# A graph network on one core: row indices of gathers copied by GpSimd, one attention product with the weights' columns, tables of pairs made in two places

## What is computed

```python
# layer 0: attention over the edges and the nodes' own loops, 4 heads of 128
alpha = leaky_relu(a_src[src] + a_dst[dst] + a_edge)
ex = exp(alpha - segment_max(alpha, dst)[dst])
out = segment_sum(h[src] * (ex / segment_sum(ex, dst)[dst])[:, :, None], dst) + bias
# layer 1: two convolutions, 256 and 512 wide
x = segment_sum((x @ W1)[src] * norm[:, None], dst) + b1     # then relu, and again with W2
# layer 2
x_neigh = segment_sum(x[src] * edge_weight[:, None], dst) / max(degree, 1)
out = x @ W_self.T + b_self + x_neigh @ W_neigh.T + b_neigh
# layer 3: the sum goes over the edges by the other end
out = segment_sum((x @ W3)[by] * edge_weight[:, None], to) + bias
```

## Time and profile before

| | |
|---|---|
| median of 3 runs | 4595.86 us (4595.8 to 4596.43) |
| the profiled execution | 4594.67 us, span 4592.7 us |
| PE busy | 3095.3 us (67%) |
| GpSimd (POOL) busy | 2949.3 us (64%) |
| VectorE (DVE) busy | 2564.1 us (56%) |
| ScalarE (ACT) busy | 1715.2 us (37%) |
| mean granted TensorE clock | 0.803 of 2.4 GHz |

### The profile page before, as it was taken

How to read it: one execution, slowest core, us unless ns; L and a number is a source line. 1 busy time by engine, 2 the same in 40 slices (tenths; PEclk the granted TensorE clock), 3 DMA queues, 4 the chain that set the end, 5 groups by cost and what they waited for, 6 DMA issues and landing times. The chain is left out here.

```text
span 4592.7 us, 69306 instructions
## 1 busy us (share of the span) xinstructions
PE 3095.3 (67%) x12429; PEld 1743.1 (38%) x12430; DVE 2564.1 (56%) x4877; ACT 1715.2 (37%) x3843; POOL 2949.3 (64%) x3208
## 2 busy tenths in 40 slices
PE   6577674487788666665545665776777799577773
PEld 6344442355556243333323333332222244222221
DVE  9456565666666663334443444665656654556556
ACT  1111110355555553333323333324444433344444
POOL 8667776666666566666666666666666667566662
PEclk8677776699998886666756666898999999789996
DMA  3211111355555153332343333325666611466663
GB/s 101 74 45 63 63 48 37 129 164 160 162 160 156 44 148 88 89 88 87 86 139 90 88 87 87 75 66 165 176 172 176 174 51 43 132 172 177 174 176 127
DMA packets 207412, 520.84 MB, mean 113 GB/s; under 512 B 63334, under 2 KB 70638, under 8 KB 206892
## 3 DMA queue, kind: packets, MB, share of 16 engines
q0 software_dynamic: 157600, 413.73, 32.3%
q1 hardware_dynamic: 49714, 105.90, 7.3%
HBM read 475.94 MB, written 43.49 MB: 113 GB/s over the span
## 5 line engine op out<-in xcount | busy, mean ns | idle before, releaser
L1554 PE MATMUL g_part<-g_rows,g_hot 128*128 x3328 | 1564.1, 619 | 868.9 <-SPq L1467 459.8
L1536 DVE TENSOR_TENSOR k_acc<-k_acc,g_part 128x256 f32 (+1 forms) x1664 | 920.3, 553 | 1046.0 <-PE g_part L1554 404.1
L1554 PEld LDWEIGHTS g_part<-g_rows,g_hot 128*128 128x128 f32 x3328 | 753.1, 245 | 1679.7 <-issue 1610.8
L1489 ACT ACTIVATE g_rows<-g_rows,k_rec 128x256 f32<-128x256 f32 (+1 forms) x1176 | 663.6, 577 | 1094.8 <-PE g_part L1554 277.0
L1166 POOL DMA_INDIRECT at_rows<-h_table,at_index x392 | 395.7, 1010 | 260.4 <-ACTq L1189 151.6
L1505 POOL DMA_INDIRECT g_rows<-support,g_index x392 | 377.2, 962 | 227.7 <-issue 125.2
L1505 POOL DMA_INDIRECT g_rows<-hidden_scaled,g_index x392 | 382.8, 977 | 212.3 <-issue 124.6
L1505 POOL DMA_INDIRECT g_rows<-x,g_index x392 | 381.8, 974 | 213.6 <-issue 124.6
L1505 POOL DMA_INDIRECT g_rows<-x_scaled_w,g_index x392 | 381.0, 972 | 208.5 <-issue 118.3
L639 POOL DMA_INDIRECT edges_by_dst<-fr_records,f_dst_slots x392 | 385.0, 982 | 167.5 <-issue 166.8
L1192 ACT ACTIVATE at_rows<-at_rows,gat_att 128x128 f32<-128x128 f32 x1176 | 373.8, 390 | 274.1 <-PE at_part L1222 120.6
(11 more groups left out here) (402 smaller groups left out, 3973.5 us busy)
## 6 DMA issues: line engine op xcount, KB each, us to landing
f_rows<-low_rows SPq DMA_DIRECT2D x28, 896.0 KB
x<-n_out SPq DMA_DIRECT2D x50, 256.0 KB
f_x_in<-in_x SPq DMA_DIRECT2D x25, 256.0 KB, 2.8
h_table<-f_h SPq DMA_DIRECT2D x25, 256.0 KB
gat_h_all<-h_table SPq DMA_DIRECT2D x5, 1280.0 KB
n_x<-in_x SPq DMA_DIRECT2D x25, 256.0 KB
n_x<-x SPq DMA_DIRECT2D x25, 256.0 KB
support<-k_acc SPq DMA_DIRECT2D x25, 256.0 KB
```

Of the source, the lines that this page charges most:

```text
L1489: act.activation(rows[:, n, :], rows[:, n, :], ACT.Copy, scale=col(rec[:, :, R_W], g * BT + (h * BT + n))).then_inc(weighed, 1)
L1536: dve.tensor_tensor(here, here, part[u % RING][:, 0:width].unsqueeze(1), ALU.add).then_inc(added, 1)
L1554: pe.matmul(part[u % RING][:, 0:width], hot[:, u % (2 * HOTS), :], rows[:, bass.ds(place[n], 1), :].rearrange("p o f -> p (o f)"), start=T ...
```

## The change

- In `aggregate`, ScalarE's index copy is gone. GpSimd copies two indices before every second gather, counts up `indexed`, waits for that count and issues the gather.
- In `aggregate` and `attention_sums`, SyncE's relay is gone. TensorE loads `T_NEED` itself, takes the need of every second pair and waits for `weighed`.
- In `attention_sums`, a slot is 521 columns wide. ScalarE copies nine weights' columns for four slots at a time behind the slots' rows (`give`, after every fourth grant), and heads 1 to 3 and the weights are one product of 393 columns; the order of PSUM columns is unchanged for the addition.
- A class `PairTable` makes one table: three marks on VectorE (narrower by the padding), the column sums on TensorE with the constants added by a product of one row, the copies into the table on ScalarE, the places on VectorE. `attention_weights` makes the dst table, spread between its other steps, with the selection behind the first large comparison; `gat_output` makes the src table at its start.
- ScalarE clears `acc` in `attention_weights`, after the rows' numbers are copied and before the ends of the scans; GpSimd did it first of all.

Cut to its core:

```diff
+class PairTable:
...
+    def mark(self, dve):
+        at, pair = self.k.columns[0:NT, :], self.w.pair
+        upto, some, less, late = (pair[:, i, self.here] for i in range(4))
+        dve.tensor_scalar(self.marks[0][:, 0:TILES], at[:, 0:TILES], upto, None, ALU.is_ge)
+        dve.tensor_scalar(self.marks[1][:, 0:TILES], at[:, 0:TILES], upto, less, ALU.is_ge, ALU.mult)
+        dve.tensor_scalar(self.marks[2][:, 0:EC], at[:, 0:EC], late, some, ALU.is_ge, ALU.mult).then_inc(self.marked, 1)
+    def sums(self, pe):
+        pe.wait_ge(self.marked, 1)
+        for i, width, first in ((1, TILES, 1), (0, TILES, None), (2, EC, 2 * BT + 1 - LAG)):
+            last = pe.matmul(self.banks[i][:, 0:width], self.k.ones[0:NT, :], self.marks[i][:, 0:width],
+                             start=True, stop=first is None)
+            if first is not None:
+                last = pe.matmul(self.banks[i][:, 0:width], self.k.ones[0:1, :], self.k.columns[0:1, first:first + width],
+                                 start=False, stop=True)
+            last.then_inc(self.summed, 1)
+    def needs(self, dve):
+        dve.wait_ge(self.summed, 1)
+        dve.tensor_scalar(self.need, self.banks[1][0:ROWS_T, 0:TILES], float(EC), None, ALU.min).then_inc(self.needed, 1)
+    def rows(self, act):
+        act.wait_ge(self.needed, 1)
+        act.copy(self.table[T_NEED:T_NEED + 1, 0:TILES], self.need[T_NEED:T_NEED + 1, :])
+        act.wait_ge(self.summed, 3)
+        act.copy(self.table[T_NODES:T_NODES + 1, 0:TILES], self.banks[0][T_NODES:T_NODES + 1, 0:TILES])
+        act.copy(self.table[T_DONE:T_DONE + 1, 0:EC], self.banks[2][T_DONE:T_DONE + 1, 0:EC]).then_inc(self.told, 1)
+    def places(self, dve):
+        dve.wait_ge(self.needed, 1)
+        dve.tensor_scalar(self.place, self.need[T_PLACE:T_PLACE + 1, :], float(BT - 1), None, ALU.add).then_inc(self.placing, 1)
+        dve.wait_ge(self.placing, 1)
+        return dve.tensor_scalar(self.table[T_PLACE:T_PLACE + 1, 0:TILES], self.place, BT - 1, None, ALU.bitwise_and)
...
             def _(pool):
-                pool.memset(acc[:, :, :], 0.0).then_inc(filled, 1)
                 pool.memset(rec[:, TILES:TILES_PAD, R_HEAD], 0.0)
                 pool.memset(rec[:, TILES:TILES_PAD, R_LOCAL], -1.0).then_inc(filled, 1)
...
-                pe.wait_ge(marked, 1)
-                for key, banks in enumerate(((p_tab, p_ends, p_carry), p_t)):
-                    for i in range(3):
-                        last = pe.matmul(banks[i][:, 0:TILES_PAD], k.ones[0:NT, :], marks(i, key), start=True, stop=True)
-                    last.then_inc(summed, 1)
+                pairs.sums(pe)
                 pe.wait_ge(loaded, 16)
                 pe.matmul(p_edge[0:R, 0:1], k.shift[0:R, 0:R], zt[:, LAST, R_DST:R_DST + 1],
                           start=True, stop=True).then_inc(before_row, 1)
-                pe.wait_ge(tabled, 2)
                 for c in range(2):
...
+                pairs.rows(act)
...
                 act.copy(rec[:, 0:TILES, R_LOCAL], p_t[2][:, 0:TILES]).then_inc(evicted_act, 1)
+                act.activation(acc[:, :, :], k.ones[:, 0:1].unsqueeze(2).broadcast_to([P, NT + 1, ACCW]), ACT.Copy,
+                               scale=0.0).then_inc(filled, 1)
                 act.wait_ge(ends_turned, 1)
...
-                c.run(dve.tensor_tensor(upto[:, :], number[:, :], p_tab[0:NT, 0:2], ALU.add))
-                for key in range(2):
-                    at, here = k.columns[0:NT, :], slice(key, key + 1)
-                    dve.tensor_scalar(marks(0, key), at, upto[:, here], None, ALU.is_ge)
-                    dve.tensor_scalar(marks(1, key), at, upto[:, here], some[:, here], ALU.is_ge, ALU.mult)
-                    last = dve.tensor_scalar(marks(2, key), at, late[:, here], some[:, here], ALU.is_ge, ALU.mult)
-                for key, (table, banks) in enumerate(((dst_table, (p_tab, p_ends, p_carry)), (src_table, p_t))):
-                    dve.wait_ge(summed, key + 1)
-                    c.run(dve.scalar_tensor_tensor(need(key), k.columns[0:R, :], 1.0, banks[1][0:R, 0:TILES_PAD], ALU.add, ALU.subtract))
-                    c.run(dve.tensor_scalar(need(key), need(key), float(EC), None, ALU.min))
-                    mine, there = slice(T_NEED, T_NEED + 1), slice(T_PLACE, T_PLACE + 1)
-                    dve.tensor_copy(table[T_NODES:T_NODES + 1, :], banks[0][T_NODES:T_NODES + 1, 0:TILES_PAD])
-                    dve.tensor_copy(table[mine, :], need(key, mine))
-                    c.run(dve.tensor_scalar(place(key), need(key), float(BT - 1), None, ALU.add))
-                    dve.tensor_scalar(table[there, :], place(key, there), BT - 1, None, ALU.bitwise_and)
-                    dve.scalar_tensor_tensor(table[T_DONE:T_DONE + 1, :], k.columns[T_DONE:T_DONE + 1, :], float(2 * BT + 1 - LAG),
-                selection(dve, k, sel, base, most[:, 0, 0:TILES], R).then_inc(chosen, 1)
+                c.run(dve.tensor_tensor(w.pair[:, 0, :], number[:, :], p_tab[0:NT, 0:2], ALU.add))
+                pairs.mark(dve)
                 dve.wait_ge(loaded, 16)
...
                 c.run(dve.tensor_tensor(top[:, :, :], edge_z, own_z, ALU.max))
+                pairs.needs(dve)
+                dve.wait_ge(pairs.needed, 1)
+                selection(dve, k, sel, base, pairs.need, R).then_inc(chosen, 1)
                 dve.wait_ge(next_row, 1)
...
                 last.then_inc(scanned, 1)
+                pairs.places(dve)
...
-    U = 2 * BT
+    U, WIDE = 2 * BT, F - C + ATT
     with Scope(nc, "at") as s:
-        rows = s.sb("rows", [P, BT, F])
+        rows = s.sb("rows", [P, BT, F + ATT])
         index = s.sb("index", [P, 2, BT], I32)
...
-                least = [sp.alloc_register(f"{s.name}_need{n}") for n in range(BT)]
-                with sp.Fori(0, TILES // BT) as i:
-                    need = at_least_one(sp, least, registers(nc, mybir.EngineType.SP, pairs, T_NEED, i * BT, 1, EC))
-                    for n in range(BT):
-                        sp.wait_ge(weighed, need[n])
-                        sp.sem_inc(arrived, 1)
...
+                def give(g, h, n):
+                    act.copy(rows[:, n:n + LAG, F:F + ATT], att[:, bass.ds(g * BT + (h * BT + n + 1), LAG), 0:ATT])
...
                         act.sem_inc(freed, 1)
+                        if n % LAG == LAG - 1 and (more or n + 1 < BT):
+                            give(g, h + (n + 1) // BT, (n + 1) % BT)
                         for hd in range(1, HEADS):
...
                         if n == 0:
                             place = registers(nc, mybir.EngineType.PE, pairs, T_PLACE, at + r, 0, BT - 1)
-                            own = registers(nc, mybir.EngineType.PE, pairs, T_NEED, at + r, 1, EC)
+                            need = at_least_one(pe, least, registers(nc, mybir.EngineType.PE, pairs, T_NEED,
+                                                                     at + r, 1, EC)[1::2])
...
                         if r % 2 == 0:
-                            pe.wait_ge(arrived, at + (r + 2))
+                            pe.wait_ge(weighed, need[n // 2])
                         pe.wait_ge(added, at + (r + 1))
-                        pe.matmul(part[r % RING][:, C:F], hot[:, matrix, :],
-                                  rows[:, bass.ds(place[n], 1), C:F].rearrange("p o f -> p (o f)"), start=True, stop=True)
-                        pe.matmul(part[r % RING][:, F:F + ATT], hot[:, matrix, :],
-                                  att[:, bass.ds(own[n], 1), 0:ATT].rearrange("p o c -> p (o c)"), start=True, stop=True)
-                        pe.matmul(part[r % RING][:, 0:C], hot_first[:, matrix, :],
+                        pe.matmul(part[r % RING][:, F:F + WIDE], hot[:, matrix, :],
+                                  rows[:, bass.ds(place[n], 1), C:F + ATT].rearrange("p o f -> p (o f)"), start=True, stop=True)
+                        pe.matmul(part[r % RING][:, F - C:F], hot_first[:, matrix, :],
                                   rows[:, bass.ds(place[n], 1), 0:C].rearrange("p o f -> p (o f)"),
                                   start=True, stop=True).then_inc(summed, 1)
...
                         here = acc[:, bass.ds(tile[n], 1), 0:F + ATT]
-                        dve.tensor_tensor(here, here, part[r % RING][:, 0:F + ATT].unsqueeze(1), ALU.add).then_inc(added, 1)
+                        dve.tensor_tensor(here, here, part[r % RING][:, F - C:F + WIDE].unsqueeze(1), ALU.add).then_inc(added, 1)
...
-                held = [sp.alloc_register(f"{s.name}_need{n}") for n in range(BT)]
-                with sp.Fori(0, TILES // BT) as i:
-                    need = at_least_one(sp, held, registers(nc, mybir.EngineType.SP, pairs, T_NEED, i * BT, 1, EC))
-                    for n in range(BT):
-                        sp.wait_ge(weighed, need[n])
-                        sp.sem_inc(arrived, 1)
...
-                def stage(g, h):
```

(15 more changed lines are left out.)

56 lines of the change are left out of this document (31 added, 25 removed).

## The result

The changed kernel takes 4814.64 us (median of 4 runs, 4801.85 to 4817.47) against 4596.15 us in the same comparison: ratio 1.0465, 95% interval 1.0442 to 1.0488. That is 218 us slower; the forecast was 4767, 171 slower, in a range of 4640 to 4890. The profiled execution took 4817.47 us (span 4815.4), 222.8 more than that of before, and the steps are judged against this difference.

The account below looks back on a forecast made before the run. GpSimd was taken to bound the four sums, 85% of them by its own work. Copies +244, attention -60 and tables -12 sum to +172, less 0.6; from 4595.9 that gives 4767 us, range 4640 to 4890.

Parts of the forecast that it names:

- The copies: Four sums: index copies moved to GpSimd lengthen its own path, +194 us plus 50 of remaining stalls, +244 us.
- 50 of stalls left: Four sums: GpSimd's stalls still remaining beside the copies, 50 us for the four, bounds 0 and 200.
- The price of 0.70: Four sums: one GpSimd copy with its wait costs 0.70 us, 137 us a stage, 549 for four.
- The relay: Removing SyncE's relay brings the four sums no gain of its own, only shorter stalls; 459.8 us of waits there.
- The attention: Attention sum: one product instead of two saves 52 us of TensorE, most of it counting; with relay and copies -60 us.
- The stage near 590: Attention sum: the whole stage was expected near 590 us, with products every 0.97 us.
- The tables: Weights' stage: VectorE starts when the records arrive, at about 784 instead of 800.67; net -12 us, bounds -5 and -16.
- The second table: Moved to the stage behind the attention: hidden in VectorE's 7.63 us wait for its first load; uncovered about 5 us.
- step 1: Four sums: index copies move to GpSimd, +244 us; contention with VectorE would add some 10 us a sum, left to the range.
- The copy is hidden: Rival, four sums: start-up behind the wait costs nothing extra, only 0.21 us a copy; kernel 4463 us, chance 0.11.
- Everything but the copies goes well: Rival: no stalls left in the sums, attention at GpSimd's own pace (-130); kernel 4646 us, chance 0.15.
- TensorE's clock falls in the wide sums: Rival: granted clock drops to 0.64 in the two wide sums, 40 us a sum, +80; kernel 4847 us, chance 0.13.

Follow-up runs that it names:

- experiment 2: Parts of the change tried singly on the kernel before (4603.78 us): index copies moved to GpSimd, 4856.21 us (1.0552); SyncE's relay removed from the sums, 4593.32 us (0.9971).
- before_again: The kernel before, unchanged, run again for its trace: 4601.02 us, ratio 0.9993 to the kernel before.
- after_again: The changed kernel, unchanged, run again: 4811.65 us, ratio 1.0449 to the kernel before.
- old_attention: The changed kernel with the attention sum of before, two products and SyncE's relay: 4704.49 us, ratio 1.1324 to the kernel before (4154.20 us).
- experiment 4: No new kernel: traces of the same four sums compared between a slower and a faster chip; g1 takes 582 against 506 us.
- two_products_no_relay: The changed kernel with two attention products, still without relay, and `acc` cleared on GpSimd again: 4713.57 us, ratio 1.1344 to the kernel before (4154.20 us).
- copy_ahead: The changed kernel with GpSimd copying each index pair one pair ahead: 4193.17 us, 1.0096 of the kernel before; repeated, 4199.50 us, 1.0104.
- act_copies: The changed kernel with the four sums' index copies back on ScalarE: 4133.72 us, 0.9954 of the kernel before; repeated, 4135.97 us, 0.9957.

## Why the prediction was right

**The copies.** Right, in kind and in size, for a chip of kind A. The start to start of 1.95 and 1.27 by turns, the 0.7 to 0.8 us of idle time (0.81), each sum 649 to 656 us, gathers still at 380 to 384 busy: all as put. Waits on ScalarE's queue at the gathers, put under 100 us, are 340.4 in the view, but they are the start-up that the view puts down to the grant. The term was +194 of own work and 50 of stalls left, 244; measured is 260.5, and +252 for the copies alone in experiment 2. The price of 0.70, read from the scatter loop, came out as 0.71. Gaps longer than the pattern (0.30, and 0.70 more for a copy) add up to some 15 us a sum, 60 in all, against 50.

The step that made the forecast come out is the one that set this price against *the stalls that the copies swallow* and not against nothing: 559 us of copies raise four sums by 260 on chip A, because 355 us of stalls (82 to 96 a sum beyond the fixed gap) nearly vanish at the slower pace. Its reason was off, though. I let each stall shrink by 1.4 us of extra room. What the traces show is that the episodes do not occur at all: of some 1,100 register and semaphore instructions of 0.6 to 0.8 us, on all engines, in the four sums of `before_again` one is left in those of `after_again`. That 50 was so near to 60 is luck. And on a chip without stalls nothing is swallowed: `old_attention` is 550 us above the kernel before, 13%, far outside the range of the forecast. That the forecast came out rests on the kind of chip on which both kernels were compared, which the prediction did not consider.

**The relay.** Right in the main: it was put at no gain of its own, only at shorter stalls. The 459.8 us of waits were worth 10 us (0.3%).

**The attention.** The mechanism was right, the size was not: -60 predicted, -23.0 measured (and 642.8 to 617.3 in experiment 2). The products' pace fell by more than was put. From one pair's first product to the next pair's it was 1.09 us as the median of the stage and is 0.88, where 0.97 was predicted (in the rows 0.89 from 1120.39 to 1121.28; behind a wait 0.99, from 1119.63 to 1120.62):

```profile
1119.63 0.92 PE L1248 MATMUL at_part<-at_rows,at_hot 128*128 x2 [0.31 <-DVE at_hot_first L1262]
1120.39 0.38 PE L1250 MATMUL at_part<-at_rows,at_hot_first 128*128 x2
1120.62 0.83 PE L1248 MATMUL at_part<-at_rows,at_hot 128*128 x2
1121.28 0.38 PE L1250 MATMUL at_part<-at_rows,at_hot_first 128*128 x2
```

To the last gather TensorE is busy 447 us, where it was 516: 70 less, where 52 was put. The step that failed is "TensorE is busy 523 of 652 us, so most of it counts". A busy share of 80% is no share of the path. In the stage of before GpSimd stood still 132 us beyond its fixed gaps of 0.30; with the product it stands 113. What these stalls of chip A come from is open (experiment 4), so why a shorter product takes so little off them is not shown. On chip B, where only 17 to 20 us of them are left, the gain is 8 to 10 us, the relay's part is none, and the stage ends at GpSimd's pace of 523, near the 515 that bounded this term. The stage near 590 was therefore wrong: 621.6.

**The tables.** Right: -12.7 against -12. Counted from the load of the records it is -12.2, and -12.3 in the repeated pair, whose first gathers are only 9.0 us apart because the stage of `after_again` begins later. VectorE's first comparison of records starts when they have arrived, at 783.68 where about 784 was put, and not at 800.67:

```profile
783.68 1.15 DVE L1088 TENSOR_TENSOR mx_same<-mx_zt 98x511 f32<-98x511 f32 x1 [10.37 <-DMA mx_zt<-edges_by_dst]
```
```profile
797.85 11.56 ACT L1042 ACTIVATE k_acc<-k_ones 128x13624 f32<-128x13624 f32 x1
809.31 0.29 ACT L1045 COPY mx_ends_f<-mx_p_ends 8x196 f32<-8x196 f32 x1
```

The clearing takes 11.56 us on ScalarE, where at most 19 was put, and the copy of the ends starts right behind it, 18.0 us after VectorE's first scan (791.35). In `two_products_no_relay`, without that clearing, it comes 16.6 us after that scan (781.96, 798.60). So the clearing delays it by 1.4 us, where 2 was taken. The second table is hidden as said: from the attention's end to g1's first gather 196.0 us became 197.8.

**The rivals.** *The copy is hidden* (4463) did not happen, but `copy_ahead` shows that it could have: another order hides it, as the rival's "for" had it. *Everything but the copies goes well* (4646): stalls did nearly go, the attention did not. *TensorE's clock falls in the wide sums* (4847): the opposite. It is granted 0.98 and 0.97 there instead of 0.93 and 0.91, and falls only in the narrow sums, from 0.64 to 0.54 and 0.53, toward the lower of its two levels, 1.2 of 2.4 GHz. There TensorE's busy time grows from 347 to 408 us in g1 with the same products and hides behind GpSimd. The Trainium skill ("TensorE: Matmul & The Clock Gate", Part 1, What's actually happening), by which activity releases the clock, agrees with the narrow sums, where the same products spread over 650 us instead of 580 had the lower clock, and not with the wide ones, where a lower busy share (72 to 62%) had the higher clock. The wide sums of `act_copies` have 0.97 too, at 78% busy. What they share with those of the change is that the long stalls are absent; whether that raises the clock was not tried.

The rule weighed beside step 1, contention of GpSimd with VectorE (the Trainium skill, "GPSIMD Engine Reference", Key points), was priced at 10 us a sum. That was too dear: in the changed kernel 68 of 784 copies last over 0.25 us, the longest 0.75, and all of them together 170 us against 149 at 0.19 each: 5 us a sum at most.

## What to carry to other kernels

Before a small operation goes onto the engine that sets a loop's pace, find in the trace what an operation followed by a wait costs there, start to start, and not its duration: here 0.7 us against 0.2. If it must go there, issue it one step ahead of its use, so that the wait is long fulfilled: the same copies then cost 0.08 us each. And a busy share is not a share of the path: the attention's 70 us less of TensorE bought 8 to 25 us, and waits of 460 us on the relay were worth 10. A gain or loss also depends on the stalls that it meets: measure on more than one chip before believing a forecast's amount.

The version to keep is the one with copies on ScalarE and the rest of the change (`act_copies`): 0.9954 and 0.9957 of the kernel before in two comparisons on chips B. It was not tried on a chip A.

## What was not expected of the hardware

- The same kernel takes 4154 or 4600 us by the chip it runs on, 11% apart, each with under 0.5% of scatter. In the four sums the difference goes with short episodes in which the sequencers of ScalarE and VectorE take 0.70 us for instructions of mostly 0.06, while GpSimd's gathers and the DMA packets keep their durations. What a change is worth depends on it: the changed kernel is 4.5 to 4.7% slower on one kind of chip and about 13% on the other (an estimate).
- On the slower kind up to nine in ten of the gathers' semaphore updates are missing from the trace (757 of 6272 left in g1 of `before_again`), on the other next to none. Whether the recording itself costs the time there is open.
- A copy on GpSimd between two indirect DMAs is free but for 0.08 us if nothing waits for it freshly; a wait straight behind it repeats the DMA's whole start-up, 0.81 us from the copy's end against 0.30 between two DMAs.
- TensorE's clock in the wide sums was higher at 62% busy time in even steps (0.98) than at 72% with pauses (0.93).
